# Slot-ordered weighted token rows, accumulating gathers, 98 low products on GpSimd, and a skip term seeded by ScalarE

## What is computed

```python
x, gate = split(xn @ W_in.T)
x = silu(causal_conv4(x))
ts, B, C = rms(split(x @ W_x.T))
dt = softplus(ts @ W_dt.T + b_dt)
state = state * exp(dt * A) + (dt * x) * B      # per token, 16 states
y = (sum over states of state * C) + x * D      # x * D is the skip term
s = (y * silu(gate)) @ W_out.T
g = silu(sum over the token's 2 experts of prob * (xn @ expert_w))
out = x_in + s * g
```

## Time and profile before

| | us |
|---|---|
| median of 3 timed runs | 1076.51 (1076.37 to 1077.35) |
| profiled execution | 1080.49 |
| its span in the trace | 1078.7 |
| VectorE busy | 1019.6 (95%) |
| GpSimd busy | 926.4 (86%) |
| TensorE matmul busy | 867.8 (80%) |
| ScalarE busy | 733.4 (68%) |
| DMA moved | 219.26 MB, mean 203 GB/s |

### The profile page before, as it was taken

One profiled execution on the slowest core, in us unless ns is written; L12 is line 12 of the kernel. 1 busy time (PEld: TensorE's weight loads), 2 busy tenths in 40 slices (PEclk: granted clock), 3 DMA queues, 4 the chain that ended last, 5 costly groups with the idle time before them and its releaser, 6 DMA issues.

```text
span 1078.7 us, 10219 instructions
## 1 busy us (share of the span) xinstructions
PE 867.8 (80%) x2756; PEld 321.2 (30%) x2756; DVE 1019.6 (95%) x1044; ACT 733.4 (68%) x1285; POOL 926.4 (86%) x365
## 2 busy tenths in 40 slices
PE   9944568898978998889846869889788998779577
PEld 6321123333323333333211223333222333223122
DVE  6779999999999989999999999899999989999998
ACT  3655556787876667777675766678778666667565
POOL 0629789998989989979898989799998988999895
PEclk9976678999999999999966879899999999879789
DMA  9345588556486666565734653865558656664814
GB/s 331 123 159 204 107 275 229 212 190 225 186 284 245 224 226 214 149 200 191 224 126 147 214 174 125 324 220 184 213 176 292 216 195 234 224 225 176 283 33 152
DMA packets 78089, 219.26 MB, mean 203 GB/s; under 512 B 15824, under 2 KB 17232, under 8 KB 71376
## 3 DMA queue, kind: packets, MB, share of 16 engines
q1 hardware_dynamic: 58096, 166.67, 45.4%
q10 hardware_dynamic: 12672, 31.46, 8.0%
q0 software_dynamic: 7264, 20.47, 6.4%
HBM read 176.85 MB, written 41.72 MB: 203 GB/s over the span
## 4 chain that ended last, share of the span: by engine, by line
DVE 43%; PE 19%; issue 14%; POOL 9%; DMA 7%; ACT 5%; SPq 2%; DVEq 0%; ACTq 0%; POOLq 0%
DVE sc_ps L1179 22%; DVE drive L1179 7%; POOL drive L572 5%; PE x_ps L1470 4%; DVE drive L1189 4%; PE f_ps L1423 3%; DMA rep<-rep_rows 3%; PE x_ps L1334 3%; POOL drive L585 2%; PE dt_ps L1398 2%; PE y_ps L1438 2%; DVE x_ps L1118 2%; DMA rep_rows<-dtu 2%; DMA w_ring<-wring 1%; ACT sc_ps L804 1%
## 5 line engine op out<-in xcount | busy, mean ns | idle before, releaser
L572 POOL TENSOR_TENSOR drive<-rep,b_all 128x2048 f32<-128x2048 f32 x127 | 575.9, 4540 | 20.3 <-DMA rep<-rep_rows 17.9
L804 ACT ACTIVATE sc_ps<-rep,a_neg 128x512 f32<-128x512 f32 x512 | 331.9, 681 | 91.6 <-DVE drive L1189 62.5
L1438 PE MATMUL y_ps<-drive,stack 128*32 128x512 f32 x1024 | 153.2, 673 | 91.3 <-DVE drive L1189 67.7
L1189 DVE TENSOR_TENSOR drive<-sc_ps,c_all 128x1024 f32<-128x1024 f32 x177 | 216.7, 1224 | 5.9
L1179 DVE TENSOR_TENSOR_SCAN sc_ps<-sc_ps,state,drive 128x512 f32<-128x512 f32 x178 | 218.3, 1272 | 1.8 <-ACT sc_ps L804 1.8
L1179 DVE TENSOR_TENSOR_SCAN sc_ps<-sc_ps,drive 128x512 f32<-128x512 f32 x176 | 205.3, 1212 | 2.7 <-ACT sc_ps L804 2.5
L585 POOL TENSOR_TENSOR drive<-drive,c_all 128x1024 f32<-128x1024 f32 x79 | 186.4, 2360 | 7.4 <-ACT state L783 7.2
L1423 PE MATMUL f_ps<-w_ring,xT_slot 128*128 128x512 f32 x368 | 172.1, 611 | 13.6 <-ACT xT_slot L816 12.9
L1398 PE MATMUL dt_ps<-xnT,w_g 128*128 128x512 f32 x232 | 129.7, 711 | 33.8 <-ACT dtu L771 33.8
L1423 PEld LDWEIGHTS f_ps<-w_ring,xT_slot 128*128 128x128 f32 x368 | 68.4, 194 | 116.6 <-issue 114.2
L1179 DVE TENSOR_TENSOR_SCAN drive<-sc_ps,state,drive 128x512 f32<-128x512 f32 x78 | 95.5, 1267 | 2.8 <-ACT sc_ps L804 2.8
(11 more groups left out here) (198 smaller groups left out, 1076.4 us busy)
## 6 DMA issues: line engine op xcount, KB each, us to landing
rep<-rep_rows SPq DMA_DIRECT2D x128, 512.0 KB, 6.9
w_ring<-wring SPq DMA_DIRECT2D x46, 1024.0 KB
rep_rows<-dtu ACTq DMA_DIRECT2D x32, 512.0 KB, 3.1
slot_rows<-y_slot ACTq DMA_DIRECT2D x46, 256.0 KB
w_g<-wg_in SPq DMA_DIRECT2D x32, 256.0 KB
w_x<-wx_in SPq DMA_DIRECT2D x24, 256.0 KB
xn_rows<-rep SPq DMA_DIRECT2D x16, 256.0 KB, 2.2
b_all<-bc_rows SPq DMA_DIRECT2D x16, 256.0 KB, 4.3
```

The source lines that it names most:

```text
L572: pool.tensor_tensor(drive[:, m % RING, :, :], rep[:, n % 2, :, 1, :], b_all[:, q:q + 1, :].broadcast_to([P, NR, TC]), ALU.mult).then_inc( ...
L804: act.activation(sc[:, r, :], rep[:, n % 2, r, 0, :], ACT.Exp, scale=a_neg[:, lo:lo + 1]).then_inc(decay_ok, 1)
L1189: dve.tensor_tensor(drive[:, m % RING, 2 * h:2 * h + 2, :], sc[:, 2 * h:2 * h + 2, :], c_all[:, q:q + 1, :].broadcast_to([P, 2, TC]), ALU. ...
L1438: last = pe.matmul(y_ps[CH * r:CH * (r + 1), :], stack[:, :], drive[:, m % RING, r, :], start=False, stop=(m % NQ == NQ - 1))
```

## The change

- **Slots.** The slots' rows now stand in HBM in slot order (`slot_x`). SyncE first fills them with zeros: 23 x 128 rows for row 0 in one DMA before the stores of `xn`, and row 1 in six parts in tiles 1 to 6. The tokens' rows are loaded (`take_first`: 8 tiles of 128 tokens into `w_out` in one DMA, before `stage_xnT`; `take_rows`: one tile twice, in each of tiles 6 to 13), scaled by ScalarE by both probabilities (`scale_rows`, 32 instructions, 16 of them in tile 0), and scattered by GpSimd (`put_rows`, 32 scatters of 128 rows). A slot is then a plain load by SyncE (`load_slot`). List, `put_in_order` and slot gathers are gone.
- **Pairs.** GpSimd gathers the first result rows and then gathers the second ones with an accumulating DMA onto them. Scaling and additions after the gather are gone.
- **Low products.** `POOL_QUADS` names 98 quads.
- **Skip.** From tile 1 on ScalarE writes `D * x` into `y_ps` and TensorE's sums add onto it. `diag` and the skip matmul are left in tile 0 only.
- The load of `w_out` waits in tile 2 for row 0's scatters. The kept outputs go through `zeros` rather than `moe`, each waiting for the store of the one before.

```diff
-FOUR_QUADS = (4, 6, 20, 22)
-POOL_QUADS = {n: (0, 1, 2, 3) if n in FOUR_QUADS else (0, 1, 2) for n in range(TILES) if 2 <= n % (PER_ROW * NT) < 14}
-POOL_QUADS[15], POOL_QUADS[30] = (0, 1), (0,)
+POOL_QUADS = {n: (0, 1, 2) if 6 <= n < 14 else (0, 1, 2, 3) for n in range(TILES) if 2 <= n % (PER_ROW * NT) < 14}
+POOL_QUADS.update({14: (2, 3), 15: (0, 1), 16: (3,), 17: (1, 2, 3), 30: (0, 3)})
...
-LATE_PUTS = [(2, 0), (2, 2), (11, 2), (12, 0), (12, 2), (13, 0), (13, 2), (13, 3)]
+CLEARS = {n: (4 * (n - 1), min(4 * n, SLOTS)) for n in range(1, 7)}
+TAKES = [6, 7, 8, 9, 10, 11, 12, 13]
+PUTS = {(0, 3): (0, 3), (1, 0): (3, 6), (1, 1): (6, 8)}
+PUTS.update({(n + (n < 13), 0 if n < 13 else 3): (RT + i, RT + i + 1) for i, n in enumerate(TAKES)})
...
+        def staged(k, s):
+            if k < RT:
+                return w_ring[:, k // HK, k % HK, :] if s else w_out[:, k, :]
+            return moe[:, 2 * (k % 2) + s, :]
...
-            sp.wait_ge(tok_zero, 1)
...
+            def clear_slots(b, lo, hi):
+                sp.dma_start(slot_x[b].rearrange("(p j) h -> p j h", p=P)[:, lo:hi, :],
+                             zeros[:, :].rearrange("p (o h) -> p o h", o=1).broadcast_to([P, hi - lo, H])).then_inc(s_zero[b], 16)
...
+            sp.wait_ge(zero_ok, 1)
+            clear_slots(0, 0, SLOTS)
...
-            def load_order(b):
...
+            def take_first():
+                sp.dma_start(w_out[:, :, :], xn_rows[0:P * RT, :].rearrange("(k p) h -> p k h", p=P)).then_inc(s_take[2], 16)
...
+            def take_rows(k):
...
+                for s in range(2):
+                    sp.dma_start(staged(k, s), xn_rows[P * k:P * (k + 1), :]).then_inc(s_take[k % 2], 16)
...
+            def load_slot(b, j):
...
+                m = SLOTS * b + j
+                if j == 0:
+                    rows_put(sp, b)
+                if m >= 2:
+                    sp.wait_ge(xt_mm, m - 1)
+                sp.dma_start(x_slot[:, m % 2, :], slot_x[b][P * j:P * (j + 1), :]).then_inc(s_gx[m % 2], 16)
...
+            take_first()
...
+                    rows_put(sp, 0)
...
-                    load_order(b)
+                    load_slot(b, 0)
...
+                if n in CLEARS:
+                    clear_slots(1, *CLEARS[n])
+                if n in TAKES:
+                    take_rows(RT + TAKES.index(n))
...
+                    load_slot(b, first_slot + 2)
...
-            def put_in_order(b, lo, hi):
...
-            def gather_slot(b, j):
...
-                    pool.wait_ge(xt_mm, m - 1)
-                pool.indirect_dma_start(x_slot[:, m % 2, :], None, xn_rows[:, :],
-                                        bass.IndirectOffsetOnAxis(ap=slot_tok[:, m:m + 1], axis=0)).then_inc(s_gx[m % 2], 16)
...
-            def gather_pairs(c, lo, hi):
+            pool.memset(zeros[:, :], 0.0).then_inc(zero_ok, 1)
...
+            def put_rows(lo, hi):
+                for k in range(lo, hi):
...
+                    pool.wait_ge(scaled, 2 * (k + 1))
+                    for s, row in enumerate((row1, row2)):
+                        pool.indirect_dma_start(slot_x[b][:, :], bass.IndirectOffsetOnAxis(ap=row[:, k:k + 1], axis=0),
+                                                staged(k, s), None).then_inc(s_scat[k % 2 if b else 2], 16)
+            def gather_first(c):
                 b = c // PER_ROW
...
+                pool.wait_ge(s_ys, 16 * SLOTS * (b + 1))
+                if c < NCH - 1:
                     pool.wait_ge(s_keep, 16 * TT * (b + 1))
...
+                    rows_put(pool, 1)
+                else:
                     pool.wait_ge(o_mm, TT * c)
...
+                for i in range(TT):
...
+                    pool.indirect_dma_start(first_rows(c, i), None, slot_rows[b][:, :],
+                                            bass.IndirectOffsetOnAxis(ap=row1[:, TT * c + i:TT * c + i + 1], axis=0)).then_inc(s_pair[c % 2][i], 16)
+            def add_second(c):
+                b = c // PER_ROW
+                for i in range(TT):
+                    pool.wait_ge(s_pair[c % 2][i], 16 * (2 * (c // 2) + 1))
+                    pool.indirect_dma_start(first_rows(c, i), None, slot_rows[b][:, :],
+                                            bass.IndirectOffsetOnAxis(ap=row2[:, TT * c + i:TT * c + i + 1], axis=0),
+                                            compute_op=ALU.add).then_inc(s_pair[c % 2][i], 16)
...
-            def combine(c, lo, hi):
...
-                    pool.tensor_tensor(moe[:, i, :], moe[:, i, :], pair_buf[i], ALU.add).then_inc(comb_ok, 1)
...
+                    gather_first(c - 1)
+                put_rows(*PUTS.get((n, 0), (0, 0)))
                 drives(NQ * n + 3)
                 low_products(NQ * n + 1)
...
+                    add_second(c - 1)
...
-                if c:
-                    act.wait_ge(s_out[i], 16 * c)
-                act.copy(moe[:, i, :], x_ps[:, :]).then_inc(s_ev, 1)
+                k = TT * (c // PER_ROW) + i
+                if k:
+                    act.wait_ge(s_keep, 16 * k)
...
+                act.copy(zeros[:, :], x_ps[:, :]).then_inc(s_ev, 1)
...
-                act.activation(diag[:, :], ident[:, :], ACT.Copy, scale=dsk[:, n % NT:n % NT + 1]).then_inc(diag_ok, 1)
...
+            def skip(n):
...
+                c, t = divmod(n, NT)
+                act.wait_ge(gated, n)
+                act.activation(y_ps[:, :], xy[:, c % 2, t, :], ACT.Copy, scale=dsk[:, t:t + 1]).then_inc(skip_ok, 1)
...
-            def scale_pairs(c, lo, hi):
...
+            def scale_rows(lo, hi):
+                for k in range(lo, hi):
...
+                    for s, prob in ((1, p2), (0, p1)):
+                        act.activation(staged(k, s), staged(k, 0 if k < RT else s), ACT.Copy,
+                                       scale=prob[:, k:k + 1]).then_inc(scaled, 1)
...
+            def silu_moe(c, lo, hi):
                 for i in range(lo, hi):
...
+                    act.wait_ge(s_pair[c % 2][i], 32 * (c // 2 + 1))
...
                 decays(m + 1, 1)
+                skip(n)
                 copy_slot_T(b, first_slot)
...
+                if n == 0:
+                    scale_rows(0, 2)
                 decays(m + 3, 0)
+                if n == 0:
+                    scale_rows(2, 5)
...
-            def combine_last(lo, hi):
...
-                    dve.tensor_tensor(first_rows(c, i), first_rows(c, i), second_rows(c, i), ALU.add).then_inc(comb_last, 1)
...
-                pe.matmul(y_ps[:, :], diag[:, :], xy[:, c % 2, t, :], start=True, stop=False).then_inc(skip_mm, 1)
+                    pe.wait_ge(skip_ok, n)
...
+                pe.matmul(y_ps[:, :], diag[:, :], xy[:, 0, 0, :], start=True, stop=False)
```

191 lines of the change are left out of this document (63 added, 128 removed).

## The result

The changed kernel takes **1079.25 us** (median of 12 runs, 1077.64 to 1082.49) against 1076.44 of the kernel before (12 runs, 1073.55 to 1081.88). The ratio is **1.0036, 95% interval 1.0021 to 1.0051**: slower by 0.36%, 3.9 us, where 20 us faster was forecast. (The two medians alone differ by 2.8 us; this text goes by the ratio.) The profiled execution took 1082.41 us with a span of 1080.6.

The account below looks back on a forecast made before the run. VectorE, 95% busy, was taken to pace the scan loop, with GpSimd nearly full. 23.8 + 1.8 + 3.8 - 5.6 - 1.3 - 1.5 - 1.0 = 20.0 us gained, so 1056.5 us was forecast, range 1049 to 1070.

Parts of the forecast that it names:

- three signs that the forecast gave for being wrong: VectorE waiting at the gate in most tiles, waits for factors in tiles 23 to 29, scan loop beginning later than 78 us.
- The seed, 1.0 us: ScalarE's 128x512 scaled copy into y's bank, per tile, in place of a 128x128 one: 1.0 us lost in all.
- The rival had the right side: Seed on the path between gate multiply and sums(4n): slower if each of 31 tiles slips above 0.75 us; chance 0.07.
- 19 x 1.25 = 23.8 us: Nineteen low products moved from VectorE to GpSimd, each worth 1.25 us off the engine setting the pace: 23.8 us gained.
- No cost: Quad 4n+3's low sums, waiting for GpSimd, end about when the next tile begins; their gate multiply stands 5.75 us behind.
- The rival that I set beside the Trainium skill's factor of about two: GpSimd becomes the bound: tiles of 18 to 29 grow, 12 us in all, giving 1068; chance 0.20.
- GpSimd's room: GpSimd takes 44.8 us of products, loses 46 slot gathers and 12 pair additions; its 10.2 us lead covers shortest tiles.
- Tile 30: GpSimd's 33.0 us of work against a 27.1 us tile uses up most of its lead: 1.5 us lost.
- Tile 25: TensorE sets this tile's length, so the moved product gains nothing and VectorE's 1.25 us turn into waiting: 1.3 us lost.
- The start, 5.6: Start loses 5.6 us: ScalarE's tile 0 copies delay decays (2.3 to 3.4), SyncE's 2 MB read delays tile 1's factor rows.
- Tile 2's 1.8 us: ScalarE's wait for slot 0's transposes in tile 2 goes, since the load is issued before the tile: 1.8 us gained.
- The tail, 3.8: Without pair additions after the last gate multiply the end comes at 1072.2: 3.8 us gained, second rows needed by about 1068.

Follow-up runs that it names:

- e9: Changed kernel, but ScalarE copies the transposed slot before writing the seed, and TensorE waits for the seed after the expert's matmuls; 0.9980 of the kernel before.
- e7: Changed kernel with the skip term back on TensorE and 89 low products on GpSimd instead of 98; 0.9935 of the kernel before.
- e1: Changed kernel with the skip matmul back on TensorE and the scaled identity on ScalarE, 98 products; 0.9971 of the kernel before.
- e8: Changed kernel with TensorE transposing the first slot six times over in tiles 4, 6, 7, 20, 22 and 23; 0.9946 of the kernel before.
- e6: Changed kernel with the skip term back on TensorE and the old table of 79 products; 0.9951 of the kernel before.
- e11_plain_second: Changed kernel with second gathers of the pairs overwriting instead of adding, for timing only; 0.9930 of the kernel before.
- e4_both: Changed kernel with the skip term back on TensorE and 91 products on GpSimd; 0.9955 of the kernel before.

## Why the prediction was wrong

None of the three signs that the forecast gave for being wrong came: VectorE waits at the gate 7 times, not in most tiles, it doesn't wait for factors in tiles 23 to 29, and the scan loop begins at 77.97. Both losses came in other places.

- **The seed, 1.0 us: measured 7.0 to 9.5.** I named what is queued behind it (copy, expert, sums) and priced its place in ScalarE's queue, but not what the skip matmul's leaving does to TensorE. It lay in the middle of a wait; without it the wait is one idle piece of 3.7 us, after which the clock was low (6.51 for 3.67 us). The copy behind the seed, which I had named, counts too (e9). The earlier trace rows show granted clocks of 0.66 and 0.60 where TensorE has little to do, and I did not ask where else it would stand. The rival had the right side (slower) with 0.07, but the wrong place: waits at the gate rose only from 9.7 to 11.4 us.
- **19 x 1.25 = 23.8 us: measured 0.3** in the changed kernel, -2.2 (noise) with the skip term on TensorE, 4.1 with the clock kept, 8.8 with plain gathers besides. The 1.25 us hold product by product where VectorE sets the pace. The step that failed is the "No cost" after "The low sums of quad 4n+3 now wait for GpSimd". I asked who needs the sums (the gate), not what stands behind them in TensorE's queue: w_g's, dt's and the output's matmuls, then ScalarE's exp of dt and VectorE's dt. The rival that I set beside the Trainium skill's factor of about two (GPSIMD Engine Reference, section Key points) came out nearer than my sum: the products pay only where GpSimd has time to spare. But it looked for the lateness in tiles 18 to 29; it is worst in 16, 17 and 30.
- **GpSimd's room.** It was counted with gathers of 0.99 us plus 0.30. The accumulating ones take 1.56 plus 0.30 and delay what follows. Tile 16 and 17's four new products, right behind eight gathers, I never costed as a place. Tile 30 was said to lose 1.5: it lost 4.2 (its wait for factors), and e7 shows that the tiles ahead had spent the lead.
- **Tile 25**: right, 31.55 us with TensorE 30.78 busy. **Tiles 26 to 29**: 1.3, 0.2, 1.3 and 0.9 shorter; 27 is off.
- **The start, 5.6: measured 3.3.** Tile 2 begins at 145.57, not 142.31. Both parts show, smaller:

```profile
102.29 9.02 POOL L588 TENSOR_TENSOR drive<-rep,b_all 128x2048 f32<-128x2048 f32 x2 [8.43 <-DMA rep<-rep_rows]
...
105.18 2.35 DVE L1182 TENSOR_TENSOR_SCAN sc_ps<-sc_ps,drive 128x512 f32<-128x512 f32 x2 [0.60 <-ACT sc_ps L801]
...
112.67 2.35 DVE L1182 TENSOR_TENSOR_SCAN sc_ps<-sc_ps,drive 128x512 f32<-128x512 f32 x2 [1.09 <-ACT sc_ps L801]
...
135.75 2.35 DVE L1182 TENSOR_TENSOR_SCAN sc_ps<-sc_ps,drive 128x512 f32<-128x512 f32 x2 [1.32 <-POOL drive L588]
```

GpSimd starts on the rows of tile 1 at 102.29, after a true wait of 8.43 us. The 98.71 of the earlier trace rows is no wait: that scatter stands behind the same gap of 0.30 as its neighbours, so it only tells about when the rows came. By it they are some 3.6 us later, not 5.9. That fits a delay by SyncE's 2 MB (the DMA engines are 0.67 busy from 90 to 105 us, 0.47 before), but no run takes this read away. ScalarE's copies cost 0.60 and 1.09 us in tile 0; GpSimd's quad 7 ends at 135.7, where I said 138.0. The scan loop starts at 77.97: the zero fill costs nothing there, as said.

- **Tile 2's 1.8 us** didn't come: other waits took their place (1.34 for decays, 1.32 for dt).
- **The tail, 3.8: measured 3.1.** From the last gate multiply's end, 1070.45, it is 7.55 us, not 10.7:

```profile
1069.76 0.69 DVE L1209 TENSOR_TENSOR xy<-y_ps,gate 128x512 f32<-128x512 f32 x1 [1.94 <-PE y_ps L1433]
...
1070.70 0.63 ACT L884 ACTIVATE xy<-xy 128x512 f32<-128x512 f32 x1 [1.21 <-DMA xy<-slot_rows,rows]
...
1076.72 1.28 DVE L1221 TENSOR_TENSOR xy<-xy,xnT 128x512 f32<-128x512 f32 x2
```

The last second rows are there at 1070.70, 0.25 us after that end. I had asked for 1068 with the gate multiply ending at 1065.39, 2.6 us after it, so they were in time. The difference between 6.9 and 7.55 is VectorE's order and one slow addition. Both last additions stand behind the last multiply, where I counted one; eleven of the other kernels take 7.40 us so. And here the first addition of the four took 1.86 us, not 0.68 (2.5 in e1, e8 and e9); why is open.

Slots, pairs, start and tail together were put at 0 and measured 5.3 us of gain (e6); tiles 13, 15 and 19 lost 1.4 to 1.9 us of waits each that I hadn't counted.

## What to carry to other kernels

A unit of work on the pacing engine is worth its duration only in stages where nothing else is near its limit; count it tile by tile, and for the engine that takes the work ask what stands in order behind each result that now comes later, not only who needs it. Before removing a matmul from a gap in TensorE's queue, look at the idle stretch that remains: here that cost 7 to 9.5 us, where ScalarE's instructions were priced at 1. Price an instruction form that the trace doesn't show (the accumulating gather) apart from its plain sibling, and first look at what stands behind it on its engine.

## What the runs showed of the hardware

- **TensorE's clock.** After 3.68 us without a matmul the next eight ran in 6.51 us, in tile 22; after 1.50 us in 3.67. It isn't a sharp rule: ahead of tile 6's expert the same 3.68 us stand in the changed kernel (then 6.44 us) and in e11_plain_second (then 3.67), and up to there the two kernels do the same. In the changed kernel alone, 3.71 us in tile 11 were followed by 3.67 us of matmuls, and 2.00 us in tile 12 by 5.37; in e4_both, with the skip matmul back in its place and only 0.36 us of gap behind it, the eight of tile 22 took 5.37. What decides it stays open, and from e11 to the changed kernel it goes with 2.0 us of tile 6's length. The Trainium skill (TensorE: Matmul & The Clock Gate, section What's actually happening) says that one kernel's count of slow matmuls differs from run to run; the traces of the changed kernel and of e11 agree.
- **Accumulating gathers** (128 rows of 512) hold GpSimd for 1.56 us where a plain one takes 0.97. After them each GpSimd instruction ended 0.57 us later than usual (5.11 for 4.53, 2.94 for 2.36 us), while starts kept their distance, for 20 to 38 us, until GpSimd next waited or issued gathers. With plain gathers not one did. The Trainium skill (Perfetto Trace Analysis, section GPSIMD Engine Instruction) holds reported GpSimd ends to be unreliable and would go by the starts, which say that nothing was lost. Here the ends were real: the factors of 610.05 end at 615.16 by their record, and VectorE, which waits for them, starts at 615.19. In the whole trace every VectorE instruction that waited for GpSimd's factors starts 0.03 us after their recorded end, and every TensorE one that waited for a low product 0.05 to 0.06 after it, late ends and usual ones alike.
